# Sixteen-head attention between two feed-forward layers: the last projections move among the first row scores, and four split residues move from VectorE to GpSimd

## What is computed

```python
ckv = x @ w_kv + b_kv
key = concatenate([ckv @ w_ku + b_ku, x @ w_kr + b_kr], axis=-1)
q_lat = x @ w_q + b_q
query = concatenate([q_lat @ w_qu + b_qu, q_lat @ w_qr + b_qr], axis=-1)
value = ckv @ w_vu + b_vu
scores = einsum('bhqd,bhkd->bhqk', q, k)          # 16 heads of 32, causal
at = softmax(scores / sqrt(32))
out = einsum('bhqk,bhkd->bhqd', at, v) @ w_o + b_o
```

## Time and profile before

| what | us |
|---|---|
| median of 3 runs | 1224.05 (1222.79 to 1225.31) |
| the profiled execution | 1222.3 |
| its span in the trace | 1220.5 |
| TensorE busy | 1081.9 (89%) |
| VectorE busy | 900.7 (74%) |
| ScalarE busy | 803.6 (66%) |
| GpSimd busy | 362.1 (30%) |
| first attention batch | about 361 to 631 |
| second attention batch | about 634 to 900 |

### The profile page before, as it was taken

One profiled execution on the slowest core, in us unless ns is written; L12 is line 12 of the kernel. 1 busy time (PEld: TensorE's weight loads), 2 busy tenths in 40 slices (PEclk: granted clock), 3 DMA queues, 4 the chain that ended last, 5 costly groups with the idle time before them and its releaser, 6 DMA issues.

```text
span 1220.5 us, 18032 instructions
## 1 busy us (share of the span) xinstructions
PE 1081.9 (89%) x5939; PEld 489.4 (40%) x5990; DVE 900.7 (74%) x2229; ACT 803.6 (66%) x1193; POOL 362.1 (30%) x388
## 2 busy tenths in 40 slices
PE   0788999998898789999999699999999799998886
PEld 0343455554444333332344233232344345554443
DVE  4788888989984888884335887884234798888893
ACT  5489888888645345666615355567547988888762
POOL 2101244444561342101210450002200133443456
PEclk9998999998999889999999899999999999999998
DMA  9200000002000221210000321100000000000000
GB/s 368 99 1 1 2 1 1 2 1 57 1 1 1 71 66 29 53 36 2 1 21 9 76 56 34 47 36 2 1 1 1 1 1 19 19 18 18 19 19 35
DMA packets 22287, 37.45 MB, mean 31 GB/s; under 512 B 5398, under 2 KB 7833, under 8 KB 21532
## 3 DMA queue, kind: packets, MB, share of 16 engines
q1 hardware_dynamic: 21404, 34.54, 9.0%
q0 software_dynamic: 768, 1.57, 0.5%
HBM read 19.17 MB, written 4.21 MB: 19 GB/s over the span
## 4 chain that ended last, share of the span: by engine, by line
PE 62%; DVE 21%; issue 7%; SPq 3%; POOL 2%; ACT 2%; DMA 1%; DVEq 1%; another core or an unknown queue 0%; POOLq 0%; ACTq 0%
PE zP L521 14%; PE oP L573 11%; PE xP L693 5%; PE oP L693 5%; PE zP L619 5%; PE zP L677 4%; PE hP L656 3%; PE hP L543 3%; DVE arena L1301 3%; DVE m L1309 3%; PE zP L718 2%; PE hP L718 2%; DVE scored L1506 2%; PE zP L656 2%; DVE arena L1382 1%
## 5 line engine op out<-in xcount | busy, mean ns | idle before, releaser
L834 ACT ACTIVATE arena<-arena,X 128x2048 int8<-128x2048 f32 x154 | 307.9, 2005 | 4.9 <-DVE X L1281 4.8
L893 ACT ACTIVATE arena<-zP,asc 128x512 f32<-128x512 f32 (+3 forms) x384 | 200.6, 582 | 108.2 <-PE zP L681 78.8
L521 PE MATMUL zP<-T,arena 128*128 128x512 f16 x1024 | 249.8, 388 | 0.9
L573 PE MATMUL oP<-T,arena 128*128 128x512 f16 x832 | 200.5, 385 | 0.9 <-DVE arena L1396 0.9
L521 PEld LDWEIGHTS zP<-T,arena 128*128 128x128 f16 x1024 | 102.3, 100 | 123.2 <-issue 12.1
L790 ACT ACTIVATE arena<-zP,sc 128x512 f32<-128x512 f32 x128 | 87.4, 687 | 93.8 <-PE zP L526 65.3
L573 PEld LDWEIGHTS oP<-T,arena 128*128 128x128 f16 x832 | 82.2, 99 | 79.6 <-issue 6.0
L677 PE MATMUL zP<-arena 98*128 98x512 f16 (+3 forms) x384 | 110.5, 334 | 2.6 <-DMA arena<-arena 1.7
L656 PE MATMUL hP<-arena 96*128 96x512 f16 (+3 forms) x256 | 84.0, 351 | 16.0 <-DVE mx L1506 12.9
L1010 POOL TENSOR_SCALAR ln<-ln 128x1 f32<-128x1 f32 x32 | 38.6, 1205 | 189.8 <-DVE ln L1221 189.6
L1506 DVE CUSTOM_DVE_ANT_0 scored<-hP,causal 128x128 bf16<-128x128 f32 (+3 forms) x170 | 80.6, 484 | 19.1 <-PE hP L656 17.8
(11 more groups left out here) (207 smaller groups left out, 1834.6 us busy)
## 6 DMA issues: line engine op xcount, KB each, us to landing
arena<-arena SPq DMA_DIRECT2D x168, 64.0 KB, 2.0
arena<-in_w_synT SPq DMA_DIRECT2D x4, 1024.0 KB, 8.1
arena<-in_w_outT SPq DMA_DIRECT2D x4, 1024.0 KB, 14.8
out_dram<-x_sb SPq DMA_DIRECT2D x16, 256.0 KB, 2.0
x_sb<-in_x SPq DMA_DIRECT2D x3, 1024.0 KB, 14.0
arena<-in_w_o SPq DMA_DIRECT2D x2, 1024.0 KB, 5.0
arena<-arena POOLq DMA_DIRECT2D x24, 64.0 KB, 1.9
arena<-in_b_syn SPq DMA_DIRECT2D x1, 1024.0 KB, 12.0
```

The costliest lines, as they stand in the source:

```text
L521: pe.matmul(zP[:, c * CW:(c + 1) * CW], part[:, g % 2, k, :], T1[:, k, c * CW:(c + 1) * CW], start=(n == 0 and k == 0), stop=False)
L573: mm = pe.matmul(o, part[:, k, :], T2[:, k, :], start=(c == 0 and n == 0 and k == 0), stop=False)
L834: act.activation(junk[:, counted[0] % 2, :], Z[:, g % ZR, :], ACT.Sign, bias=X[:, 2, k:k + 1], accum_out=S[:, k:k + 1]).then_inc(sm["cnt"], 1)
L893: act.activation(PT[:, m // 4 % 2, h, q0:512], colP[m % 3][:, q0:512], ACT.Exp, scale=asc[:, g, 10:11]).then_inc(sm["exp_done"], 1)
```

## The change

Seven things change, in each batch:

1. ITEMS has a new order: in 0/1, up 0, up 2, in 2, up 1, up 3, in 3, up 4, up 5 (two items each), then the values. `project` stops after item 13 (`IN_CORE`); the items 14 to 19 (in 3, up 4, up 5) and the values 20 to 27 are elements `item` of ORDER.
2. VectorE does the low parts 0 and 1 early, after the peak of item 8; the peaks of items 14 to 19 are elements `peak` of ORDER, with `scale` of groups 2 and 3 behind them.
3. ScalarE's `split_hi` of groups 1, 2 and 3 are elements `hi` of ORDER.
4. The first unit has the items 14 to 19 and the low parts 2 and 3 among its row scores (`opening`).
5. The second unit has the values, the peaks 16 to 19 and the high parts of groups 2 and 3 among its row scores (`behind_opening`); the turn of the first unit stands after three row scores as before. From the row scores of head 3, query tile 4, on, ORDER is what it was.
6. The low parts 4 to 7 are GpSimd's, two instructions each (multiply in place, subtract), after its four `all_max`.
7. GpSimd's first memset of constant rows stands ahead of its `all_max` and no longer behind them.

```diff
+IN_CORE = 14
+FIRST_VAL = 20
+def opening(rows):
+    r = iter(rows)
+    def take(n):
+        return [next(r) for _ in range(n)]
+    order = [("hi", 1), ("item", 14)] + take(4) + [("peak", 14), ("item", 15), ("lo", 2)] + take(4) + [("lo", 3)]
+    order += [("item", 16), ("item", 17)] + take(2) + [("peak", 15), ("item", 18)] + take(2) + [("item", 19)] + take(4)
+    return order
+def behind_opening(rows, turn):
+    r = iter(rows)
+    order = [("item", 20), ("item", 21)]
+    for n in range(3):
+        order += [next(r)] + [("item", 22 + n)] * (n < 2)
+    order += [turn, ("item", 24), ("peak", 16), ("peak", 17), next(r), ("item", 25), next(r), ("item", 26), ("hi", 2)]
+    order += [next(r), ("item", 27), ("peak", 18), ("peak", 19), next(r), next(r), ("hi", 3)]
+    return order + list(r)
...
             def project(b):
+                pool.wait_ge(*((sm["a_rstd"], BT) if b else (sm["x_new"], NT)))
+                unit_rows(b, 0)
                 for g in range(GROUPS):
                     all_max(b, g)
+            def split_lo(b, m):
+                k, w = SPLITS[m]
+                pool.wait_ge(sm["split_hi"], 8 * b + m + 1)
+                link(pool.tensor_scalar(qk[:, w, k, :], qk[:, w, k, :], asc[:, k, 8 + w:9 + w], None, ALU.mult))
+                pool.tensor_tensor(parts[:, k, w, 1, :], qk[:, w, k, :], parts[:, k, w, 0, :], ALU.subtract)                    .then_inc(sm["split_lo"], 1)
...
             def core(b):
-                for g in range(3):
+                for m in range(4, 2 * KD):
+                    split_lo(b, m)
+                for g in (1, 2):
```

More of the change, by code:

```diff
@@ L58, in core_order @@
             unit.sort(key=lambda e: e[2])
-            others = [[("val", n)] + ([("lo", n + 3)] if 1 <= n <= 4 else []) for n in range(BT)]
-            unit = [e for n in range(BT) for e in others[n] + unit[2 * n:2 * n + 2]]
+            unit = opening(unit)
+        elif (g, qc) == (0, 1):
+            unit = behind_opening(unit, turn)
+            turn = None
         if turn:
@@ L67, in core_order @@
     for u in units:
-        start[u] = min(len(rows), rows.index(("turn", *u)) + 1 + LEAD)
+        lead = [n for n, e in enumerate(rows) if e[0] == "row" and n > rows.index(("turn", *u))]
+        start[u] = lead[LEAD - 1] + 1 if len(lead) >= LEAD else len(rows)
     ends = [0]
@@ L281, in program @@
         ITEMS = [("in", j, tc) for tc in range(2) for j in (0, 1)]
-        ITEMS += [("up", j, tc) for j in (0, 2, 1, 3, 4, 5) for tc in range(2)]
-        ITEMS += [("in", j, tc) for j in (2, 3) for tc in range(2)]
-        VALUES = len(ITEMS)
+        for kind, j in (("up", 0), ("up", 2), ("in", 2), ("up", 1), ("up", 3), ("in", 3), ("up", 4), ("up", 5)):
+            ITEMS += [(kind, j, tc) for tc in range(2)]
+        assert len(ITEMS) == FIRST_VAL
         ITEMS += [("val", i, 0) for i in range(BT)]
@@ L295, in program @@
         COMPLETE = [max(n for n, e in enumerate(ITEMS) if plane(e) and plane(e)[1] == g) for g in range(GROUPS)]
-        TOTAL = {k: seen(k, len(ORDER)) for k in ("row", "max", "turn", "col", "mix", "norm", "rec", "mix_v", "val", "lo")}
+        TOTAL = {k: seen(k, len(ORDER)) for k in ("row", "max", "turn", "col", "mix", "norm", "rec", "mix_v")}
         RING = [e for e in ORDER if e[0] in ("row", "turn")]
@@ L601, in project @@
                 pe.wait_ge(sm["aw_in"], 16 * 3 * KD)
-                for n in range(VALUES):
+                for n in range(IN_CORE):
                     if (b, n) == (0, 2):
@@ L636, in core @@
                     kind, g = e[:2]
-                    stack = stacks[STACK_OF[g]] if g < GROUPS else None
+                    stack = stacks[STACK_OF[g]] if kind in ("row", "col") else None
                     if kind in ("row", "turn"):
@@ L641, in core @@
                             pe.wait_ge(*free)
[L642 to L645, removed]
+                    elif kind == "item":
+                        item(b, g)
+                    m = n.get(kind, 0)
+                    n[kind] = m + 1
                     if kind == "row":
@@ L1068, in core @@
                         wait_stack(pool, b, 1)
-                    pool.memset(stacks[g][3 * HD:3 * HD + 2, 1, :, :], MUNIT).then_inc(sm["unit_set"], 1)
-                    pool.wait_ge(sm["unit_set"], 3 * b + g + 1)
+                    unit_rows(b, g)
                 pool.wait_ge(sm["bo_in"], 16 * (b + 1))
@@ L1454, in project, with peak @@
             def project(b):
[L1455 to L1458, removed]
+                for n in range(IN_CORE):
+                    if plane(ITEMS[n]):
+                        peak(b, n)
                     if ITEMS[n] == ("in", 2, 0):
-                        for m in range(4):
+                        for m in range(2):
                             split_lo(b, m)
[L1462 to L1468, removed]
+            def peak(b, n):
+                w, g, tc = plane(ITEMS[n])
+                dve.wait_ge(sm["p_out"], b * len(ITEMS) + n + 1)
+                step(dve.tensor_reduce(mxq[:, g, w, tc:tc + 1], qk[:, w, g, tc * 512:(tc + 1) * 512],
+                                       AX.X, ALU.max, apply_absolute_value=True))
+                if n in COMPLETE:
+                    after(0)
+                    dve.tensor_reduce(asc[:, g, 0:2], mxq[:, g, :, :], AX.X, ALU.max).then_inc(sm["p_max"], 1)
+                    scale(b, g)
             def scale(b, g):
@@ L1498, in core @@
                         split_lo(b, g)
+                    elif kind == "peak":
+                        peak(b, g)
                     if kind == "row":
```

25 lines of the change are left out of this document (14 added, 11 removed).

## The result

The median went from 1223.42 (1222.74 to 1225.31, 4 runs) to **1247.26** (1246.31 to 1248.05, 4 runs), a ratio of 1.0205 [1.0183, 1.0228]. (One more run of the kernel before has moved its median from 1224.05 to 1223.42.) That is 23.8 slower, where +32.7 and 1256.8 were forecast. The span of the profiled execution is 1245.2, 24.7 longer.

The account below looks back on a forecast made before the run. TensorE was taken to bound the kernel outside the attention openings, VectorE within them. 16.6 + 15.5 - 1.7 - 2.7 + 5.0 = +32.7 on 1222.3 gives 1255.0, plus 1.75 for the median: 1256.8; range 1241 to 1271.

Parts of the forecast that it names:

- One of the signs that were named: Sign of a right forecast: GpSimd's low-part instructions L1088 and L1089 stand on the profile page's chain of waits.
- The opening: Start of each attention batch: second batch's last all-reduce ends at 689.3, first column score at about 692, 7.7 earlier.
- The gap: GpSimd reconfiguration between its last all-reduce and first low part, counted as 7.0 of waiting; lower bound 0.
- The pairs: GpSimd's two instructions per low part: 5.35 to 5.8 a pair, taken as 5.55; four pairs 22.2.
- The loads: Loads of stack 1 behind the last low part: 9.9 from SyncE's first issue to all landed.
- The sum: Delay of `row.1000`, first row score of group 1: 16.6 later in the second batch, 15.5 in the first.
- What follows it: Effects behind the wait for stack 1: -1.7, -2.7 and +5.0 over both batches.
- The turn's wait: TensorE's wait of 0.86 at the turn behind `row.1000` goes, in both batches alike: -1.7.
- the bias adds: On GpSimd, no longer behind a reconfiguration, they end before the next unit's maxima are due: -2.7.
- The clock: TensorE at granted 0.50 for some 8 behind `row.1000` after idling: 2.5 a batch, +5.0.
- The hold rival: No gap behind GpSimd's reconfiguration; its low parts hold VectorE's scale 3; `row.1000` at 722.9, time 1245.8; chance 0.13.
- The rival that the gain comes through: Stack 1 is there when TensorE is (704); both batches start columns some 8 earlier: 1208; chance 0.04.

Follow-up runs that it names:

- kernel 1: Changed kernel with low parts 4 to 7 back on VectorE and GpSimd's gone, all else as changed: 1215.43, ratio 0.9949.
- 3: Kernel before the change with only low parts 4 to 7 moved to GpSimd, behind its first memset: 1232.07, ratio 1.0097.
- 6: Changed kernel with GpSimd doing keys' low parts 5 and 7, then loads of stack 1 waiting only for these, then 4 and 6: 1229.85, ratio 1.0066.
- kernel 4: Changed kernel with GpSimd's low part 4 put between its all-reduces of groups 2 and 3: 1264.53, ratio 1.0359.
- kernel 7: Kernel 1 with the first memset back behind the all-reduces, so only the new order is left: 1222.71, ratio 1.0010.
- kernel 5: Changed kernel with keys' low parts 5 and 7 on VectorE, GpSimd's 4 and 6 behind its loads, stack 1 waiting for keys' parts only: 1210.34, ratio 0.9911.

## Why the prediction was right

The forecast chain is what happened, and the rivals fell: kernels 1, 3 and 6 show that GpSimd's low parts are the loss, kernel 4 that the gap is a price of the switch. One of the signs that were named can't be read: the page's chain of the changed kernel breaks off after 1% of the span, so whether L1088 and L1089 are on it is seen from the timelines alone. Its steps, second batch:

- **The opening.** Last all-reduce at 34.0 behind scale 0 forecast, 33.1 measured (700.24 less 667.17). First column score at 36.7 behind scale 0 forecast (692 less 655.34), 35.5 measured, so 8.9 earlier for the forecast 7.7. 3.4 of it is the memset (38.4 in kernel 7, 35.1 in kernels 1 and the change, at the wait ahead of it); the rest is the order.
- **The gap** was forecast at 7.0 from the earlier trace rows and measured at 6.72 and, in the first batch, 7.45. The Trainium skill, GPSIMD Engine Reference, section 2.1 Instruction dispatch, gives about 6 for the first call after a load; every gap into arithmetic here was longer, only the ones into the all-reduce (5.79 and 6.03) are near it.
- **The pairs** were mis-sized: "I take 5.55, the middle, as nothing speaks for an end". Measured 20.1 for four, 5.03 each, 2.1 less in sum, and below the low bound of 5.35. tensor_scalar was at its low bound (2.85; 2.89 given), tensor_tensor under it (2.12 to 2.14; 2.35 given). That bound took off only the fixed part of a one-column instruction and kept f32 output; this one writes f16. Which of the two it is, no run separates.
- **The loads** took 10.2 from the first issue to `row.1000` (9.9 forecast).
- **The sum.** +13.7 for the forecast +16.6 (pairs 2.1, opening 0.9 and gap 0.3 less, loads 0.3 more). In the first batch, behind scale 0, +12.5 for +15.0, which is the forecast's 15.5 without the 0.5 for the first memset. Scale 0 itself ends 1.15 later there (386.02 for 384.87), but not for the memset: 1.04 of it is there before the attention begins (GpSimd ends the feed-forward layer at 374.17 for 373.13), and GpSimd waits 6.72 for VectorE between the memset and the first all-reduce.
- **What follows it** was forecast at +0.6 and is -2.6: the span is 24.7 longer, of which 26.2 is ahead of `row.1000` and the 1.15 ahead of scale 0. The turn's wait went, and the bias adds start at once, as the steps said. The clock was oversized: "for some 8 behind `row.1000`". The windows of the changed kernel (length, PE, PEld, DVE, ACT, POOL busy, granted clock, DMA share, GB/s):

```profile
720.00:724.00 4.00, 0.00 (x0) 0.00 (x0) 0.00 (x0) 0.00 (x0) 4.00 (x2) 0.50 0.00 0
736.00:740.00 4.00, 2.67 (x16) 0.87 (x17) 0.81 (x6) 0.08 (x1) 3.58 (x2) 0.50 0.32 96
740.00:744.00 4.00, 3.90 (x29) 1.50 (x27) 1.77 (x10) 1.50 (x5) 3.92 (x4) 0.55 0.01 2
744.00:748.00 4.00, 4.00 (x45) 1.48 (x38) 2.59 (x9) 2.65 (x6) 4.00 (x4) 1.00 0.39 99
```

  The granted clock is at the lower level (0.50, 1.2 GHz) in the idle time and until about 743.5, so some 6 behind `row.1000`, and only part of that is time in which TensorE is busy. In the first batch it is some 4 (0.50 up to 460.00, 0.84 in the next 1.00, 1.00 behind it). What is left for the clock in the two batches is 1.8 of the 5.0 (-2.6 + 1.7 + 2.7), a remainder and not a measurement.
- **The hold rival** was priced at 1245.8, nearer to the measured 1247.26 than the forecast's 1256.8, and `row.1000` at 70.2 lies between its 67.6 (722.9 less 655.34) and the forecast's 73.1. So the number alone would not have told the two apart. The timelines do: the gap of 6.72 and 7.45 is there, and scale 3 runs at 700.28 in instructions of 0.17, done 5.5 before GpSimd's first L1088. That the time came out near this rival's is chance: the forecast's terms were mis-sized mostly in one direction (pairs 4.2, opening 1.9 and clock 3.2 too much). The result lies 9.5 under the forecast, outside its own "some 8 either way", and in the stated range only because that was widened for this rival.
- **The rival that the gain comes through** needed the last low part 12.6 behind the last all-reduce; it was there 26.9 behind it. What kernel 5 shows is that a gain needs no faster GpSimd, only that the load doesn't wait for it: there `row.1000` stands 7.3 and 6.2 earlier than in the kernel before.

## What to carry to other kernels

Before work goes to an engine with time to spare, look at who waits for its result: here 20 of work and a switch of 7 went to an engine that is idle two thirds of the time, but between a maximum that comes last and a load that holds the bounding engine. Ask which parts that load really needs: with the keys' parts on VectorE and the load waiting for these alone, half of the GpSimd work, put behind the load, did not hold it up (kernel 5, 1210.34). And a mixture of edits is best taken apart at once: a memset of 3.51, moved by a few lines, was worth more than the new order of the projections (7.3 in the new order and 3.9 in the old one; the order alone +1.0).

## What was not expected of the hardware

- Going back from arithmetic to the all-reduce costs GpSimd 5.79, too (kernel 4); in the trace of before only one direction lay open. In the kernel before, this time lay between memset and bias adds; it costs only where GpSimd's next result is awaited.
- GpSimd's arithmetic holds VectorE too, but not always for the whole instruction. In the changed kernel these two small instructions meet it; the L1089 at 714.95 ends at 717.07, and the L1088 behind it runs from 717.04 to 719.88:

```profile
716.58 0.51 DVE L1561 TENSOR_SCALAR mm_<-mm_ 128x16 f32<-128x16 f32 x1
717.13 1.06 DVE L1565 CAST mrow<-mm_ 128x16 f16<-128x16 f32 x1
```

  In kernel 1, with GpSimd idle, they take 0.17 and 0.18. The first ends at 717.09, with L1089 (in the first batch at 436.55, L1089 at 436.53), as if it had waited for all of it. The cast was delayed by 0.9, but was over long before the 2.84 of L1088 were. The Trainium skill, SBUF — State Buffer, section SBUF: two separate sides, has the shared port locked for a whole instruction. The first row and the 3.56 of the scale instruction beside the memset (again in both batches of kernels 3 and 7) agree with it; the cast doesn't, or one of the two needs no lock. No run here tells which.
